# Weight sums made by VectorE alone, a shorter 1/std, and the front's steps placed anew

## The reference, cut to what matters

```python
def reference(x, ctx, g_xattn, g_ffn, time_decay, time_first, W1, W2, W3):
    # _wkv: per channel a recurrence over the 256 tokens; with decay exp(-exp(time_decay)),
    # y_t = weighted mean of past values v and of the token's own, weights exp(k)
    x = x + tanh(g_xattn[0]) * _wkv(time_decay, time_first, layernorm(x), ctx)
    h = layernorm(x)                                   # the second norm, over the 512 channels
    up_gate, up_lin = h @ W1.T, h @ W3.T               # 512 -> 2048, twice
    hidden = fwht(silu(up_gate) * up_lin)              # normalized Walsh-Hadamard over 2048
    return x + tanh(g_ffn[0]) * (hidden @ W2.T)
```

## Time and profile before

| | us |
|---|---|
| median of 3 runs | 1139.82 (1139.08 to 1140.48) |
| the profiled execution | 1142.86 |
| its span | 1141.0 |

### The profile page before, as it was taken

How to read it: one execution, slowest core, us unless ns; L and a number is a source line. 1 busy time by engine, 2 the same in 40 slices (tenths; PEclk the granted TensorE clock), 3 DMA queues, 4 the chain that set the end, 5 groups by cost and what they waited for, 6 DMA issues and landing times.

```text
span 1141.0 us, 18280 instructions
## 1 busy us (share of the span) xinstructions
PE 1023.8 (90%) x6892; PEld 688.7 (60%) x6892; DVE 858.4 (75%) x1315; ACT 396.8 (35%) x685; POOL 375.0 (33%) x278
## 2 busy tenths in 40 slices
PE   5698968667798999999899899999899999999998
PEld 2364423245576776666667576667667666677775
DVE  7847997868778886898778786888778986664334
ACT  6755331131422541233423341234422442232221
POOL 0133868645742115221341115221341114211111
PEclk9998998878899999999999999999999999999999
DMA  9967427346464445264354445264454442344341
GB/s 344 342 232 286 173 98 283 129 148 221 148 240 161 147 169 207 85 231 184 119 215 167 150 159 210 75 240 171 135 213 167 170 163 90 132 148 184 148 148 38
DMA packets 40909, 201.74 MB, mean 177 GB/s; under 512 B 8944, under 2 KB 18288, under 8 KB 29808
## 3 DMA queue, kind: packets, MB, share of 16 engines
q1 hardware_dynamic: 40816, 200.52, 47.9%
HBM read 171.12 MB, written 29.38 MB: 176 GB/s over the span
## 4 chain that ended last, share of the span: by engine, by line
issue 34%; PE 26%; DVE 10%; POOL 8%; DMA 2%; ACT 1%; POOLq 0%; DVEq 0%; SPq 0%; ACTq 0%
PE pl L721 3%; PE pl L723 3%; PE pl L722 3%; POOL work L1633 3%; PE po L733 3%; PE po L735 3%; PE pg L721 3%; PE pg L723 3%; PE pg L722 3%; POOL bv L1556 2%; PE po L744 1%; PE po L742 1%; DVE work L1400 1%; DMA factor_rows<-tiny 1%; DVE x L1331 1%
## 5 line engine op out<-in xcount | busy, mean ns | idle before, releaser
L1633 POOL TENSOR_TENSOR work<-work 128x512 bf16<-128x512 f32 x112 | 146.4, 1309 | 567.3 <-DVE work L1482 567.3
L733 PE MATMUL po<-work,w 128*128 128x512 f16 x456 | 173.3, 380 | 1.7 <-DVE x L1331 0.7
L735 PE MATMUL po<-work,w 128*128 128x512 f16 x456 | 172.9, 379 | 0.0
L1024 ACT ACTIVATE work<-work 128x256 f32<-128x256 f32 x168 | 68.1, 415 | 271.8 <-DVE work L1400 271.6
L721 PE MATMUL pg<-wts 128*128 128x256 f16 x448 | 124.0, 277 | 24.1 <-DVE work L1400 24.1
L721 PE MATMUL pl<-xn,wts 128*128 128x256 f16 x448 | 123.9, 277 | 0.0
L723 PE MATMUL pg<-wts 128*128 128x256 f16 x448 | 123.9, 277 | 0.0
L722 PE MATMUL pg<-wts 128*128 128x256 bf16 x448 | 123.9, 277 | 0.0
L721 PE MATMUL pl<-wts 128*128 128x256 f16 x448 | 123.9, 276 | 0.0
L722 PE MATMUL pl<-xn,wts 128*128 128x256 bf16 x448 | 123.8, 276 | 0.0
L723 PE MATMUL pl<-xn,wts 128*128 128x256 f16 x448 | 123.7, 276 | 0.0
(11 more groups left out here) (196 smaller groups left out, 2296.4 us busy)
## 6 DMA issues: line engine op xcount, KB each, us to landing
wts<-up_stage SPq DMA_DIRECT2D x56, 2048.0 KB, 8.1
up_stage<-wts SPq DMA_DIRECT2D x8, 1024.0 KB, 7.4
up_stage<-wts SPq DMA_DIRECT2D x16, 512.0 KB, 3.3
ev<-ctx_t SPq DMA_DIRECT2D x7, 1024.0 KB, 5.7
xin<-x_t SPq DMA_DIRECT2D x7, 1024.0 KB, 4.9
bv<-x_tok SPq DMA_DIRECT2D x7, 1024.0 KB, 7.1
out_t<-x SPq DMA_DIRECT2D x7, 1024.0 KB, 4.4
wts<-w_t SPq DMA_DIRECT2D x11, 512.0 KB, 6.4
```

The lines of the kernel that those rows point to most:

```text
L733: pe.matmul(po[:, d, :], w2h[:, j, d * P:d * P + P], hh[:, b, :], start=start, stop=False, skip_group_check=True)
L735: pe.matmul(po[:, d, :], w2l[:, j, d * P:d * P + P], hh[:, b, :], start=False, stop=False, skip_group_check=True)
L1024: act.activation(sg[:, slot, cols], src, ACT.Silu).then_inc(acted, 1)
L1633: pool.tensor_tensor(hl[:, b, :], hf[:, slot, :], hh[:, b, :], ALU.subtract).then_inc(pair_lo, 1)
```

## The change

**Weight sums.** POOL's `weight_sums`, `weight_sums_lo` and DVE's `wsum_hi_of` go. A new `weight_sums` on DVE makes a unit whole, in five instructions: one subtraction of 512 columns (two of the old four, by rearranged patterns), two of 256, the clamp, the low part. Units 0 to 6 stand beside slots 3, 5, 9, 10, 10, 11, 13; units 7, 8, 9 in pairs 0, 1, 2 of run 2, then two each in pairs 3, 4, 5, ahead of the joins. The raw units 13, 14, 15 are split at slots 9, 10, 11 instead of 6, 7, 8, the last two in places 4 and 5, so that the residual waits for 10 raw units, the channel sum for 13 and the variance for all 16. SP's one-off part is reordered to match.

**1/std.** DVE adds eps (`var_plus_eps`), ACT makes Ln and then Exp with scale -0.5 (`rstd_guess`, `rstd_begin`), DVE does one Newton step (`refine`): four DVE instructions instead of eleven.

**Places in a run of pairs.** On DVE all four `with_token` of the denominator stand in p1 and all of the numerator in p2; `over` and both `over_last` in p3 ahead of the joins; the residual of batch 0 in p3, of batch 1 in p4; the token moments (`tok_moments_of`) move from p5 to p6, between `var_plus_eps` and `refine`. On ACT `logs` moves from p2 to the end of p1, `rstd_guess` to the end of p5, `rstd_begin` between the two copies of p6. POOL's `quotient` moves from p3 to p2. On PE `var_full` moves behind `part` 3 and 4 of p5. `spread_factors` keeps its place in SP's step 5.

```diff
-SUMS_AT = {3: 0, 4: 1, 5: 2, 6: 3, 7: 4, 9: 5, 11: 6, 13: 7, 14: 8, 15: 9}
-LATE_SUMS = {0: (10, 11), 1: (12, 13), 2: (14, 15)}
-LATE_LO = {0: (9, 10), 1: (11, 12), 2: (13, 14), 3: (15,)}
+SUMS_AT = {3: (0,), 5: (1,), 9: (2,), 10: (3, 4), 11: (5,), 13: (6,)}
+LATE_SUMS = {0: (7,), 1: (8,), 2: (9,), 3: (10, 11), 4: (12, 13), 5: (14, 15)}
...
-        unit_slot = {0: (4,), 1: (5, 6), 2: (7, 8), 3: (9,), 4: (10, 11), 5: (12,), 6: (13,), 7: (14,), 8: (15,)}
+        unit_slot = {0: (4,), 1: (5, 6), 2: (7, 8), 3: (9,), 4: (10, 11), 5: (12,), 9: (13,), 10: (14,), 11: (15,)}
...
                 high_downs(run, p, 0)
                 if front and p == 4:
                     mean_full(front_of(run))
-                if front and p == 5:
-                    var_full(front_of(run))
                 for w in range(2):
                     pe.wait_ge(joined, g * 6 + (3 + w))
                     part(run, p, 3, w, fifth[w], False, True)
                     part(run, p, 4, w, chain[w], False, True).then_inc(product[4][w], 1)
+                if front and p == 5:
+                    var_full(front_of(run))
...
+            def rstd_guess(run):
+                act.wait_ge(newton, run.nth_full(0, X1_STEPS))
+                act.activation(rstd, var_eps, ACT.Ln).then_inc(rstd_log, 1)
+
+            def rstd_begin(run):
+                act.wait_ge(rstd_log, run.nth_full(0, 1))
+                act.activation(rstd, rstd, ACT.Exp, scale=-0.5).then_inc(rstd_first, 1)
...
+            def weight_sums(n):
+
+                b = unit_blocks(n)
+                dve.wait_ge(traw_loaded[n % TRAWS], 16 * (n // TRAWS + 1))
+
+                dve.tensor_tensor(b[:, 0:2, :].rearrange("p k (s n) -> p s k n", s=2),
+                                  b[:, :, P:].rearrange("p (s k) n -> p s k n", s=2),
+                                  b[:, 0:2, :].rearrange("p k (s n) -> p s k n", s=2), ALU.subtract).then_inc(wsum, 1)
+                dve.wait_ge(wsum, 3 * n + 1)
+                dve.tensor_tensor(b[:, 2:4, P:], b[:, 2:4, P:], b[:, 0:2, 0:P], ALU.subtract).then_inc(wsum, 1)
+                dve.wait_ge(wsum, 3 * n + 2)
+                dve.tensor_tensor(b[:, 2:4, 0:P], b[:, 2:4, 0:P], b[:, 2:4, P:], ALU.subtract).then_inc(wsum, 1)
...
                     if front and p == 5:
                         centre(ahead)
+                    if front and p == 6:
+                        var_plus_eps(ahead)
                         if more:
                             tok_moments_of(front_of(ahead))
-                    if front and p == 6:
-                        rsqrt(ahead)
+                        refine(ahead)
...
                     if front and p == 1:
-                        with_token(ahead, ea, eb, scan_b, den_done, range(0, 2))
+                        with_token(ahead, ea, eb, scan_b, den_done)
                     if front and p == 2:
-                        with_token(ahead, v, bv, scan_a, num_done, range(0, 2))
+                        with_token(ahead, v, bv, scan_a, num_done, range(2, 4))
                     if front and p == 3:
-                        over_last(ahead, 1)
+                        residual(ahead, 0)
```

More of the change, by code:

```diff
@@ L531, in _ @@
             load_again(4)
-            put_plain(6)
+            load_v(2)
             put_sums(2)
             load_again(5)
[L535 to L540, removed]
             load_x(2)
             load_tokens(2)
+            put_plain(6)
+            for n in range(3, 5):
+                put_sums(n)
+                load_again(n + TRAWS)
+            put_plain(7)
             put_sums(5)
@@ L983, in ffn @@
                         squares(ahead)
+                    if at(j, "rsqrt"):
+                        rstd_guess(ahead)
+                        rstd_begin(ahead)
                     if at(j, "norm"):
@@ L1045, in pairs @@
                     pair_silu(run, p, 5, 0, 1)
+                    if front and p == 1:
+                        logs(ahead)
+                    if front and p == 5:
+                        rstd_guess(ahead)
                     if front and p == 6:
@@ L1236, in over_last, with residual @@
                                          op1=ALU.mult).then_inc(y_done, 1)
-            def residual(run):
+            def residual(run, b):
                 if run.is_front(2):
-                    dve.wait_ge(raw_lo, UNITS)
+                    dve.wait_ge(raw_lo, 10)
                 elif not run.half:
@@ L1248, in residual @@
                     dve.wait_ge(gains, 2)
[L1249 to L1252, removed]
-                                             op1=ALU.add).then_inc(x1_done, 1)
+                dve.wait_ge(y_done, run.before + (1 if run.half else b + 1))
+                dve.scalar_tensor_tensor(out=batch_cols(x1[:, run.par, :, :], b), in0=batch_rows(bv, b),
+                                         scalar=gt[:, 0:1], in1=batch_cols(xin, b), op0=ALU.mult,
+                                         op1=ALU.add).then_inc(x1_done, 1)
             def turned_lo(b):
@@ L1414, in pairs @@
                     if front and p == 2:
-                        with_token(ahead, ea, eb, scan_b, den_done, range(2, 4))
                         scan(ahead, v, bv, scan_a)
+                        with_token(ahead, v, bv, scan_a, num_done, range(0, 2))
                     if front and p == 3:
-                        with_token(ahead, v, bv, scan_a, num_done, range(2, 4))
                         over(ahead)
                         over_last(ahead, 0)
+                        over_last(ahead, 1)
                     if front and p == 4:
-                        residual(ahead)
+                        residual(ahead, 1)
                     if front and p == 5:
                         centre(ahead)
+                    if front and p == 6:
+                        var_plus_eps(ahead)
                         if more:
                             tok_moments_of(front_of(ahead))
-                    if front and p == 6:
-                        rsqrt(ahead)
+                        refine(ahead)
                     if front and p == 7:
@@ L1432, in pairs @@
                         sums_lo(ahead, 0)
+                    if run.is_front(2):
+                        for n in LATE_SUMS.get(p, ()):
+                            weight_sums(n)
                     if begun:
@@ L1441, in pairs @@
                     join(run, p, 7, 1, early1[:, 1, T:], 1, 1)
-                    if run.is_front(2) and p in (0, 1, 2, 3):
-                        for n in {0: (9, 10), 1: (11, 12), 2: (13, 14), 3: (15,)}[p]:
-                            wsum_hi_of(n)
                     if front and p == 0:
@@ L1513, in _ @@
             over(b)
-            residual(b)
+            residual(b, 1)
             dve.wait_ge(put[0], 16)
@@ L1537, in channel_sum @@
                 if which == 0:
+                    if run.is_front(2):
+                        pool.wait_ge(raw_lo, 13)
                     pool.wait_ge(x1_done, run.done)
```

91 lines of the change are left out of this document (41 added, 50 removed).

## The result

The changed kernel takes 1168.96 us (median of 4 runs, 1167.54 to 1171.86), the kernel before 1139.45 in the same session (4 runs, 1134.94 to 1140.48): 29.5 us slower, ratio 1.027 with a 95% interval of 1.0234 to 1.0306. Forecast were 1149.0 and a range of 1121 to 1171. The direction came as forecast, and so did the wait that was to cause it; the size did not: +29.5 instead of +9.3.

A forecast was written before the change was run, and what follows sets the result against it. PE bounds the pairs (14.35 us each), DVE the stage ahead. -17 (chunk 0) - 13.2 + 1.7 + 17.7 (run 2) + 27 (runs 3 to 6) - 6.9 (run 7) = +9.3: median 1139.8 to 1149, range 1121 to 1171.

The forecast's parts named there:

- the late load: SP's queue: factor write leaves 7.0 us into p6, so pair 7 starts 28.5 after p6, not 14.5, in five runs.
- the stage ahead of run 2: Chunk 0, from 103 us: weight sums on DVE, less stretching; PE's first pair at 212.5, 17 us earlier.
- the steady runs: Runs 3 to 6: +15.2 in p6 and p7, -7.8 from front steps, +7.4 each; +27 together. Run 7: -6.9.
- 1/std is hidden: p6: ACT's added Ln, Exp and table loads, 5 us, cost PE nothing, or 0.3 if not hidden.
- the term for p4 and p5 of run 2: Joins start 10.7 and 11.3 us into the pairs; together 34.6 us instead of 32.9, +1.7.
- POOL's stretching: Chunk 0: DVE instructions lengthened by overlapping POOL's, estimated at 36 us, of which 25 go.
- rival 3: A weight-sum unit on DVE costs 5.0 us and overlaps worse: 1168 us; chance 0.16 together with rival 4.
- p0 to p3 of run 2: First four pairs of run 2, with weight-sum units ahead of joins: 74.3 us, 13.2 less.
- the forecast's own sign of being wrong: Pair 7 starts within 20 us of p6, or pairs of run 2 before p6 grow beyond 22 us.
- Rival 1: Gains outrun the late load: write takes 9.2, load 8.1, chunk 0 gains 27; 1120 us; chance 0.20.
- Rival 2: Factor write is long only through work beside it and lands in 2.2 us in p6: 1102 us; chance 0.03.
- Rival 4: p3's wait returns because POOL's quotient ends too late: +3 a run, 1164 us; chance 0.16 together with rival 3.

The follow-up runs named there:

- e1: Changed kernel with SP's load of pair 7 issued ahead of `spread_factors` in step 5: 1086.73 us, ratio 0.9557 to the kernel before.
- e2: Kernel before with only the token moments moved from p5 to p6, ahead of 1/std: 1208.39 us, ratio 1.0618.
- e7: e4 with the weight sums as before the change, on POOL, in old places and old SP order: 1097.41 us, ratio 0.9642.
- e4: Changed kernel; SP's step 5 only loads pair 7, step 6 issues factor write, next pair 0's load, then waits and spreads: 1088.73 us.
- e5: e4 with the nine late weight-sum units of run 2 split ahead of and behind DVE's joins: 1076.14 us, ratio 0.945.
- run 6: Not a follow-up: a run of eight pairs inside the kernel, last of the four (3 to 6) that together take 510.7 us before, 539.5 after.
- e8: e4 with POOL's two channel sums of run 2 cut to 8 columns (result not the reference's): 1078.71 us, ratio 0.9494.
- e9: Changed kernel with the factor write as 128 pieces of 32 bytes instead of 1024 single floats (result not the reference's): 1120.64 us.

## Why the prediction was right and where it was wrong

**Right: the late load.** Forecast: write 7.0 us into p6, a trip of 11.6, pair 7 28.5 after p6, pair 7 itself 16.4. Measured in run 3: 7.1, 10.48, 27.1, 16.19. It comes five times, as said, though in run 2 the wait is 18.9 and not 12 to 15; e1 takes the cause away and the loss with it.

**Right, with luck in the size: the stage ahead of run 2.** First pair forecast at 212.5, seen at 211.92 with a wait of 4.60 us for DVE's last blocks instead of 12.78. A unit was put at 3.6 and takes 3.56. But the first pair's start varies from execution to execution: with the sums on POOL it is 229.94 before, 224.61 in e2 (the same code up to there) and 223.26 in e7; with the sums on DVE it is 210.62 to 216.57 in the traces. The forecast started from the latest of the three. e7 gives the price on e4's base, 11 us at the first pair and 8.7 in the median; that the full 17 belongs to the change is not shown.

**Right in kind: the steady runs.** p3 and p5 gain, runs 3 to 6 take 539.5 (forecast 538), run 7 118.9 (117.3). The forecast's own terms, four runs of +7.4, make 29.6 and not the 27 that it put into the sum; measured are 28.8. That is two misses which cancel: p6 and p7 lose 55 us over the four runs where 4 x 15.2 = 61 were forecast, and p0 to p5 gain 26.5 where 4 x 7.8 = 31 were. p3 is 15.66, not 14.35: a new wait of up to 1.3 us (5 times, 5.7 in all) for DVE's instruction at L1521, because POOL's quotient, moved to p2, runs beside the end of p2 on DVE. It is the small form of what e5 shows, and most of the 1.6 us that run 7 misses. The instruction of DVE at the end of run 3's p2:

```profile
424.63 2.13 DVE L1508 TENSOR_TENSOR work<-work 128x256 f32<-128x256 f32 x1
```

The same instruction at the end of p1 takes 0.41. The clock adds to the shortfall: p3 lost 4.5 us to its wait and the clock in three of the four runs before, and 2.8 in run 6, where the clock stayed up. 1/std is hidden as forecast: Exp on ACT ends at 477.08, 5.4 us into p6, ahead of the copy that was due, and PE loses nothing.

**Wrong: the term for p4 and p5 of run 2.** "p4 and p5 34.6 instead of 32.9" measured 42.98, so +10.1 instead of +1.7; this is 8.4 of the 15.4 us by which the traces exceed the sum. The step that failed is "p4: one residual 1.7, two units: 10.7" and "p5: centring 2.35, two units: 11.3", where both take a unit at 3.6 and put what POOL does beside it at nothing. The joins started 14.0 and 13.9 us into the pairs: unit 12 took 7.5 and unit 15 took 6.2, because POOL's channel sums of x and of its square start just there. I had counted POOL's stretching as a cost that goes (25 us, chunk 0), and not asked what is left of POOL's work in run 2 and which of DVE's instructions the change puts beside it. e8 removes the sums on e4's base, where the same pairs take 42.72, and gets 7.1 us back. The forecast held POOL's channel sum in view only as something that PE waits for. The row that could have warned stands in the earlier trace rows: the 1.53 that rival 3 took for a possible price of the shape is such a stretch. POOL's instruction beside it ends at 495.73, and 0.68 more is 496.41; DVE's L1290 ends at 496.29:

```profile
494.20 1.53 POOL L1633 TENSOR_TENSOR work<-work 128x512 bf16<-128x512 f32 x1 [0.36 <-DVE work L1482]
```

**Wrong by less:** p0 to p3 of run 2, 77.2 for 74.3: the second scan took 5.4 instead of 4.4 and `over_last` 3.2 instead of 2.5 (both beside POOL), which pushed the joins to 12.5 in p2 and 15.2 in p3 (forecast 11.3, 13.8). p3 came to 23.30 us, so the forecast's own sign of being wrong, a pair of run 2 beyond 22 us before p6, was met. And PE is busy 1.7 to 2.8 us longer in p2 to p5 than in the same pairs of run 3, at the lower clock, where I added 1 to 1.9, and none in p4. p6 and p7, 49.7 for 47.9: two puts of sums stand between spread and load (350.62) and the load leaves 6.6 later, not 3.

**The 5 us that no step holds.** The medians differ by 29.5 and the traces by 24.7; the forecast passed from one to the other by taking off the same 3 us, while after's own profiled execution lay under its median. Why one execution differs from another is open. The first stage varies by itself: with identical code up to there, the first pair starts at 229.94 before and at 224.61 in e2.

**The rivals.** Rival 1 (write 9.2, load 8.1) did not come: the write took 10.5, the load 9.1. Rival 2 asked for a write of 2.2 us in p6; e9 shows that this exists, but for a write in larger pieces and not for this one. Rival 3 had a unit at 5.0 everywhere: the total came near its 1168, by another cause, two units of nine in two pairs. Rival 4 had p3's wait back because the quotient ends too late; a wait came back at under half of its size (1.1 to 1.3 us), and not because the quotient is late but because it holds up DVE's instruction at the end of p2.

## What to carry to other kernels

When a producer is moved later, walk down the queue that consumes it and list everything that stands behind its wait: here one semaphore wait in SP's queue turned a 52 us gain into a 29 us loss, and two swapped lines got it back (e1). When work moves to DVE, lay it beside POOL's timeline first: price each DVE instruction that takes two inputs from SBUF, and the clamps too, not by its length alone but by when POOL's current instruction ends. And when a small transfer takes ten microseconds, count its pieces before its bytes.

## What the hardware showed

**DVE and POOL hold each other out for whole instructions.** So these two do not meet only at semaphores, as was said at the start. In the fences of e8 every long DVE length is POOL's end plus the length alone: L1374 ends at 293.64, POOL's L1653 at 293.10 and 0.68 more is 293.78; L1378 ends at 296.13, for 295.85 + 0.42 = 296.27; L1380 at 297.54, for 297.26 + 0.42 = 297.68. All three are the same 0.14 early. In e5 L1522 ends at 274.54, for 273.99 + 0.68 = 274.67.

It seems to work the other way too: POOL's sum of 128x1024 takes 2.08 as L1593 at 318.43 and 2.79 as L1587 at 293.06, where L1374 runs until 293.64. The clamp, with one SBUF input, is held as well: L1526 at 289.67 takes 1.22 and ends at 290.89, for POOL's 290.61 + 0.43 = 291.04, 0.15 early; alone it takes 0.43, and 56 of its 112 cases are long in this way, all within 0.15 of that sum. Not affected are the joins that read PSUM and one SBUF operand (0.41 at 269.99, in the midst of POOL's quotient).

The Trainium skill ("SBUF — State Buffer", "Who interferes with whom") states this as a rule: a DVE instruction with two SBUF inputs and a GpSimd one that reads SBUF exclude each other, the first to start has the ports for its whole length, and the other fully blocks. The trace agrees within 0.14 us in each of the two-input cases above. With the lengths alone and the places of POOL's instructions, unit 12's 7.5 us could have been estimated before.

**The price of pieces.** 4 KB as 1024 single numbers: 9.2 to 12.4 us over the twelve trips before and after; as 128 pieces of 32 bytes: 1.4 to 1.7, and once 4.9. The Trainium skill ("DMA: Bandwidth & Descriptors", "Rules for kernel authors") says that a last dimension that is not contiguous becomes one descriptor per element. The trace agrees in kind (896 packets less for each write in e9), and gives the price that the prediction could take only from the earlier trace rows. The fixed cost of about 2.0 us that the prediction quotes from the same page is given there for transfers that GpSimd issues, while SP issues these; it fails for the first form, and the second comes near it.

**The clock.** After 12.50 us of idle PE starts at its lower level: the first product of pair 7 takes 0.39 where others take 0.27, the granted clock of p7 is 0.88, and PE, without one wait, takes 16.19 for 14.35. The pairs of run 2 (p1, p3, p4 and p5 in the changed kernel):

```profile
227.93:246.08 18.15, 15.18 (x109) 10.17 (x108) 17.80 (x27) 3.80 (x9) 2.31 (x2) 1.00 0.64 236
...
265.78:289.08 23.30, 17.33 (x110) 11.72 (x108) 19.15 (x27) 3.44 (x8) 4.23 (x2) 0.85 0.65 228
289.08:310.26 21.18, 17.05 (x111) 11.71 (x110) 16.82 (x23) 3.44 (x8) 7.31 (x4) 0.92 0.72 270
310.26:332.06 21.80, 16.92 (x111) 11.58 (x110) 17.54 (x26) 6.53 (x10) 6.07 (x5) 0.92 0.22 89
```

In p3, p4 and p5 PE idles 5.97, 4.13 and 4.88 us, shows a clock of 0.85 to 0.92 and is busy 1.7 to 2.8 us longer than in the same pairs of run 3. So such a wait costs more than its length. With shorter waits it differs from case to case: in p1 PE idles 2.97 us here and keeps its clock, while the same pair of e4 idles 2.98, shows 0.91 and is busy 16.85 instead of 15.18. What decides between the two is open.
